# Graph network on one core: the first layer's sender rows gathered unscaled during the degree histogram, into a ring in SBUF

## What is computed

```python
h = relu(layernorm(x))
out_deg = clip(zeros(n).at[src].add(1), 1);  in_deg = clip(zeros(n).at[dst].add(1), 1)
agg = zeros_like(h).at[dst].add((h * out_deg ** -0.5)[src])
x = x + agg * in_deg ** -0.5

h = relu(layernorm(x))
n = ln(mlp(h));  e = ln(mlp(edge_attr_8))
for s in range(2):
    e = e + ln(mlp(concat([e, n[src], n[dst]])))
    agg = segment_sum(e, dst)
    n = n + ln(mlp(concat([n, agg])))
out = x + mlp(n)
```

## Time and profile before

| | |
|---|---|
| Median of 3 runs (lowest, highest) | 12392.23 us (12387.93, 12393.55) |
| Profiled execution: span | 12392.1 us |
| PE busy | 9269.5 us (75%) |
| PEld busy | 6879.9 us (56%) |
| DVE busy | 5309.1 us (43%) |
| ACT busy | 5441.9 us (44%) |
| POOL busy | 8911.3 us (72%) |
| Mean granted TensorE clock | 0.701 of full speed |
| HBM read, written | 616.95 MB, 249.33 MB |

### The profile page before, as it was taken

One profiled execution on the slowest core, in us unless ns is written; L12 is line 12 of the kernel. 1 busy time (PEld: TensorE's weight loads), 2 busy tenths in 40 slices (PEclk: granted clock), 3 DMA queues, 4 the chain that ended last, 5 costly groups with the idle time before them and its releaser, 6 DMA issues. The chain is left out here.

```text
span 12392.1 us, 209313 instructions
## 1 busy us (share of the span) xinstructions
PE 9269.5 (75%) x60787; PEld 6879.9 (56%) x60787; DVE 5309.1 (43%) x10581; ACT 5441.9 (44%) x8544; POOL 8911.3 (72%) x9488
## 2 busy tenths in 40 slices
PE   5687888788888867777777777776667677777776
PEld 4576666677777755555555555554444444444444
DVE  8844444444444434444444444443333333333333
ACT  1144444444444434444444444444444444444444
POOL 1277777777777767777777777776777777777776
PEclk8755555555555567777778788777777777777777
DMA  2122222222222223333334444442233333333332
GB/s 79 21 38 37 37 37 37 37 41 44 44 44 44 44 69 96 96 96 96 96 97 104 103 104 104 104 101 70 70 70 70 70 70 71 73 73 73 73 73 62
DMA packets 1513870, 857.80 MB, mean 69 GB/s; under 512 B 1044173, under 2 KB 1204574, under 8 KB 1512881
## 3 DMA queue, kind: packets, MB, share of 16 engines
q1 hardware_dynamic: 1115074, 571.64, 17.4%
q0 software_dynamic: 302816, 231.81, 11.7%
q10 hardware_dynamic: 95408, 47.86, 1.4%
HBM read 616.95 MB, written 249.33 MB: 70 GB/s over the span
## 5 line engine op out<-in xcount | busy, mean ns | idle before, releaser
L1803 POOL DMA_INDIRECT edge_blk_g<-sender_part,edge_blk_lst x6256 | 5909.6, 945 | 2000.4 <-issue 1904.5
L1403 POOL DMA_INDIRECT fl_gx<-sender_x,fl_lst x3128 | 2953.7, 944 | 1375.5 <-issue 951.9
L1859 PE MATMUL edge_blk_hps<-ident,edge_blk_g 128*128 128x128 f32 x6256 | 1244.4, 361 | 2066.6 <-DMA edge_blk_g<-sender_part,edge_blk_lst 2065.3
L1859 PEld LDWEIGHTS edge_blk_hps<-ident,edge_blk_g 128*128 128x128 f32 x6256 | 1058.8, 255 | 2818.4 <-DMA edge_blk_g<-sender_part,edge_blk_lst 2796.8
L1875 ACT ACT_TABLE_LOAD x1564 | 2006.6, 1283 | 60.2 <-ACTq L966 32.0
L1889 ACT ACTIVATE edge_blk_h<-edge_blk_hps,vecs 128x512 f32<-128x512 f32 x782 | 537.3, 687 | 2885.2 <-PE edge_blk_hps L1859 2875.2
L1948 DVE SCALAR_TENSOR_TENSOR agg<-edge_blk_aggps,vecs,agg 64x64 f32 x1564 | 442.3, 283 | 3102.6 <-PE edge_blk_aggps L1819 2641.8
L1854 PE MATMUL edge_blk_hps<-edge_blk_oha,edge_blk_win 128*128 128x512 f32 x1564 | 1137.9, 817 | 30.1 <-DMA edge_blk_win<-receiver_part 30.1
L1842 PEld LDWEIGHTS edge_blk_yps<-w_edge_blk,edge_blk_h 64*128 64x128 f32 x12512 | 1000.7, 239 | 244.2 <-issue 244.2
L1842 PE MATMUL edge_blk_yps<-w_edge_blk,edge_blk_h 64*128 64x64 f32 x12512 | 1122.7, 333 | 0.0
L1451 PE MATMUL fl_aggps<-fl_ohb,fl_gx 128*96 128x64 f32 x6256 | 1072.5, 365 | 13.8 <-DMA fl_gx<-sender_x,fl_lst 13.8
(11 more groups left out here) (279 smaller groups left out, 11497.4 us busy)
## 6 DMA issues: line engine op xcount, KB each, us to landing
edge_blk_e<-edge_state SPq DMA_DIRECT2D x782, 256.0 KB
edge_state<-fl_e SPq DMA_DIRECT2D x391, 256.0 KB
edge_blk_dlb<-local_dst SPq DMA_DIRECT2D x1564, 64.0 KB
edge_blk_g<-sender_part,edge_blk_lst POOLq DMA_INDIRECT x6256
edge_state<-edge_blk_new SPq DMA_DIRECT2D x391, 256.0 KB, 3.1
fl_gx<-sender_x,fl_lst POOLq DMA_INDIRECT x3128
edge_blk_win<-receiver_part SPq DMA_DIRECT2D x1564, 16.0 KB
fl_attr<-attr_slots SPq DMA_DIRECT2D x391, 32.0 KB
```

The source lines that it names most:

```text
L1403: pool.indirect_dma_start(out=gx[n.b][:, j % TILES, j // TILES, D:D + X_DIM], out_offset=None, in_=xg_d, in_offset=bass.IndirectOffsetOnAx ...
L1803: pool.indirect_dma_start(out=g[n.b][:, i, 64 * c:64 * c + 64], out_offset=None, in_=ps_d, in_offset=bass.IndirectOffsetOnAxis(ap=lst[n.b] ...
L1859: ins = nc.tensor.matmul(h_ps[n.half][:, P * i:P * i + P], g[n.b][:, i, :], ident[:, :], start=False, stop=i == TILES - 1)
```

## The change

**Order of the stages.** `load_weights` moves from GpSimd's part of `edge_lists` to its part of the set-up. The set-up writes `hx` to memory unscaled (`normed_x`), and the block ends only when that has landed. `scaled_senders` is gone; its arithmetic stands at the end of `edge_lists`.

**Lists.** The transposed source numbers and local destinations stay in SBUF for all rounds (`idx_all`, i32, and `loc_all`, bf16). `tile_lists` is gone with its stores and with all loads of lists, in layer one and in both edge steps.

**Ring.** `gr` holds 64 rounds of gathered rows. GpSimd fills it during `edge_lists`: rounds 0 to 47 out of the unscaled table, as soon as their block's lists exist, rounds 48 to 61 out of the scaled one, once that is in memory. In layer one it goes on from round 62, and from round 64 on it waits for the slot. A new step `take` on VectorE copies a round from the ring to `gx`. GpSimd's loops are unrolled over all rounds.

**Lookup.** The first 48 rounds have to be scaled in SBUF. Their digits are stored as bf16, and each round's are spread over the partitions by two DMAs. VectorE compares the high digits with the partition's number (`hot`), TensorE multiplies the result with the 98 x 128 table of factors, split into three bf16 parts (`look`, six matmuls of 512 columns), VectorE picks by the low digit (`pick`), TensorE sums over partitions with a column of ones (`total`, eight f32 matmuls), and every 16 rounds VectorE multiplies the ring's rows with the factors (`scale`).

```diff
+RING = 64
+LIST_BLOCKS = 3
+EARLY = LIST_BLOCKS * BLOCK_E // ROUND
+AHEAD = 62
+def every_round(pool, body, count_sb, first=0):
+    for n in range(first, FAST_ROUNDS):
+        body(n)
+    sort = pool.value_load(count_sb[0:1, 0:1], min_val=0, max_val=1)
+    with pool.If(sort > 0):
+        for n in range(FAST_ROUNDS, MAX_ROUNDS):
+            body(n)
+
+def gather_sender_x(pool, n, gr, idx_all, table, g_in):
+    if n >= QUAD:
+        pool.wait_ge(g_in[n % QUAD], n // QUAD * 128)
+    for j in range(8):
+        pool.indirect_dma_start(
+            out=gr[:, n % RING, j, :], out_offset=None, in_=table,
+            in_offset=bass.IndirectOffsetOnAxis(ap=idx_all[:, 8 * n + j:8 * n + j + 1].bitcast(U32), axis=0),
+        ).then_inc(g_in[n % QUAD], 16)
...
 # set-up
-                    sp.wait_ge(s_zeros, 64)
+                    sp.wait_ge(s_hx, 1)
+                    sp.dma_start(xh_d.rearrange("(p q) c -> p q c", q=P), hx[0:NHI, :, :]).then_inc(s_zeros, 16)
+                    sp.wait_ge(s_zeros, 80)
...
+                    pool.wait_ge(s_clear, len(zero_list))
+                    load_weights(pool)
...
 # edge_lists, GpSimd
-                load_weights(pool)
+                for n in range(AHEAD):
+                    if n < EARLY and n % per_block == 0:
+                        pool.wait_ge(lists_ok, n // per_block + 1)
+                    elif n == EARLY:
+                        pool.wait_ge(lists_ok, LIST_BLOCKS + 1)
+                        pool.wait_ge(rows_out, 32)
+                    gather_sender_x(pool, n, gr, idx_all, xh_d if n < EARLY else xg_d, g_in)
...
 # edge_lists, SP
+                def spread(r):
+                    if r >= 3:
+                        sp.wait_ge(picked_ok, r - 2)
+                    sp.dma_start(hi_bc[r % 3][0:NHI, :], digit_d[1, r:r + 1, :].broadcast_to([NHI, ROUND])).then_inc(bc_in[r % 3], 16)
+                    sp.dma_start(lo_bc[r % 3][:, :], digit_d[0, r:r + 1, :].broadcast_to([P, ROUND])).then_inc(bc_in[r % 3], 16)
...
 # edge_lists, VectorE, behind the histogram
+                def hot(r):
+                    dve.wait_ge(bc_in[r % 3], r // 3 * 32 + 32)
+                    if r >= 2:
+                        dve.wait_ge(z_ok, r - 1)
+                    v.tensor_scalar(hi_hot[r % 2][0:NHI, :], hi_bc[r % 3][0:NHI, :], part_f[0:NHI, 0:1], None,
+                                    ALU.is_equal).then_inc(hot_ok, 1)
+                def pick(r):
+                    dve.wait_ge(z_ok, r + 1)
+                    if r >= 2:
+                        dve.wait_ge(fac_ok, r - 1)
+                    v.scalar_tensor_tensor(picked[r % 2], lo_bc[r % 3][:, :], part_f[:, 0:1],
+                                           z_ps[r % 2][:, :, :].rearrange("p c e -> p (c e)"), ALU.is_equal, ALU.mult).then_inc(picked_ok, 1)
+                def scale(k):
+                    dve.wait_ge(fac_ok, per_block * k + per_block)
+                    for b in range(QUAD):
+                        dve.wait_ge(g_in[b], per_block // QUAD * (k + 1) * 128)
+                    rows = gr[:, per_block * k:per_block * k + per_block, :, :].rearrange("p r j c -> p (r j) c")
+                    v.tensor_tensor(rows, rows, fac_ps[k % 2][:, 0:P].rearrange("p (r j) -> p r j", j=1).broadcast_to([P, P, X_DIM]),
+                                    ALU.mult).then_inc(scaled, 1)
...
 # edge_lists, TensorE, behind the histogram
+                def look(r):
+                    pe.wait_ge(hot_ok, r + 1)
+                    if r >= 2:
+                        pe.wait_ge(picked_ok, r - 1)
+                    for c in range(2):
+                        for i in range(3):
+                            ins = nc.tensor.matmul(z_ps[r % 2][:, c, :], r_parts[0:NHI, i, :], hi_hot[r % 2][0:NHI, CHUNK * c:CHUNK * c + CHUNK],
+                                                   start=i == 0, stop=i == 2)
+                    ins.then_inc(z_ok, 1)
+                def total(r):
+                    pe.wait_ge(picked_ok, r + 1)
+                    k, at = r // per_block, 8 * (r % per_block)
+                    if k >= 2 and at == 0:
+                        pe.wait_ge(scaled, k - 1)
+                    for j in range(8):
+                        ins = nc.tensor.matmul(fac_ps[k % 2][:, at + j:at + j + 1], picked[r % 2][:, P * j:P * j + P], one_f[:, :],
+                                               start=True, stop=True)
+                    ins.then_inc(fac_ok, 1)
...
 # first_layer
-                    landed(sp, g_in, n.back(4), 128)
-                    held(sp, passed)
-                    wait(sp, oh_ok, n.back(4))
-                    sp.dma_start(lst[n.b][:, :], lists_d[bass.ds(n.n, 1)].rearrange("a p c -> (a p) c")).then_inc(list_in[n.b], 16)
...
+                def body(n):
+                    if n >= RING:
+                        pool.wait_ge(take_ok, n - RING + 1)
+                    gather_sender_x(pool, n, gr, idx_all, xg_d, g_in)
+
+                every_round(pool, body, count_sb, AHEAD)
...
+                def take(n):
+                    landed(dve, g_in, n, 128)
+                    held(dve, passed)
+                    v.tensor_copy(gx[n.b][:, :, :, D:D + X_DIM].rearrange("p i c d -> p c i d"),
+                                  gr[:, bass.ds((n.m & (RING // QUAD - 1)) * QUAD + n.b, 1), :, :].rearrange(
+                                      "p a (c i) d -> p (a c) i d", i=TILES)).then_inc(take_ok, 1)
...
                     finish(n.back(4))
+                    take(n.back(3))
...
 # edge_step
-                    indices(n)
                     operands(n.back(2))
                     store(n.back(6))
```

More of the change, by code:

```diff
@@ L121, in held @@
     eng.sem_inc(passed, 1)
-def rounds(eng, body, count_sb, first=1):
-    quads = load_count(eng, count_sb, "quads")
-    for m in range(first):
-        for b in range(QUAD):
-            body(Slot(m, b))
-    with eng.Fori(first, quads) as m:
-        for b in range(QUAD):
-            body(Slot(m, b))
-    return Slot(quads, 0)
+def every_round(pool, body, count_sb, first=0):
[13 more added lines that the diff above has]
+        ).then_inc(g_in[n % QUAD], 16)
 def rounds_and_nodes(eng, body, count_sb, first=1):
@@ L698, in edge_lists @@
         GT = 16
-        NHI = -(-(N_NODES + 1) // P)
         G = P // GT
@@ L755, in _ @@
                 store(blocks - 1)
-                sp.wait_ge(lists_out, blocks * 32)
+                sp.wait_ge(digits_out, LIST_BLOCKS * 32)
+                for r in range(3):
+                    spread(r)
+                for k, q in enumerate(half_cols):
+                    sp.wait_ge(rows_ok, k + 1)
+                    sp.dma_start(xg_d.rearrange("(p q) c -> p q c", q=P)[:, q, :], hx[0:NHI, q, :]).then_inc(rows_out, 16)
+                for r in range(3, EARLY):
+                    spread(r)
+                sp.wait_ge(lists_out, blocks * 16)
                 held(sp, passed)
+                sp.wait_ge(rows_out, 32)
             @block.scalar
@@ L832, in _ @@
                 blocks = load_count(dve, count_sb, "blocks")
-                body(0)
-                with dve.Fori(1, blocks) as k:
+                for k in range(LIST_BLOCKS):
+                    body(k)
+                with dve.Fori(LIST_BLOCKS, blocks) as k:
                     body(k)
@@ L840, in _ @@
+                hot(0)
+                for r in range(EARLY):
+                    if r + 1 < EARLY:
+                        hot(r + 1)
+                    pick(r)
+                    if r % per_block == 2 and r > per_block:
+                        scale(r // per_block - 1)
+                scale(LIST_BLOCKS - 1)
+                dve.wait_ge(scaled, LIST_BLOCKS)
             @block.tensor
@@ L1697, in _ @@
                     normed(last.back(k))
+                    take(last.back(k + 1))
                     add_sums(last.back(k + 2))
                     finish(last.back(k + 2))
+                take(last.back(1))
                 for k in (2, 1):
@@ L1796, in _, with body @@
             def _(pool):
[L1797 to L1800 removed]
+                def body(n):
+                    if n >= QUAD:
+                        pool.wait_ge(pre, n - QUAD + 1)
                     for j in range(8):
```

290 lines of the change are left out of this document (143 added, 147 removed).

## The result

| | before | after |
|---|---|---|
| Median (lowest, highest), 4 runs each | 12391.86 us (12387.93, 12393.55) | 12214.11 us (12201.35, 12236.74) |
| Profiled execution: span | 12392.1 us | 12207.6 us |
| Round 0, round 390 of layer one | 534.5, 4402.0 | 890.6, 4242.1 |
| First gather of the first edge step | 4483.7 | 4308.7 |

The ratio is 0.9859, 95% interval 0.9847 to 0.9871: 178 us less where 72 were forecast. The direction was right and the time lies in the range, at its lower end; the gain is two and a half times the forecast one. The profiled execution has 2.1 us outside its span.

What follows compares the result with a forecast made beforehand. GpSimd's gathers were taken to bind all three layers at 9.99 us a round. Gains of 418 and 8 us less 354 for the later round 0 gave 72 us less, 12,320 us from 12,392; range 12,190 to 12,450.

Steps and rivals of the forecast that it cites:

- Round 0: Start of layer one: at 888, 354 us later than before, as GpSimd must first issue 62 rounds of gathers.
- one gather a pair: Histogram: one gather passes with each pair of one-hots, plus one a block, 225 in all; chance 0.45.
- a cover of 7.0: Lookup of 48 rounds, 5 us each, hides under GpSimd's remaining gathers, which leave 7.0 us a round.
- Rivals 1 to 3: Histogram gathers: 1, starved, 12,539 us, chance 0.12; 2, no bf16 conflict, 12,213, 0.10; 3, in between, 12,256, 0.13.
- Part 1: Layer one: engines run at their own pace, 8.70 then 8.97 us a round, 3449 us against 3867.5; gain 418 us.
- rival 4: Layer one: TensorE gets 2.4 GHz and GpSimd's 3287 us bind; 162 us less, 12,158; chance 0.07.
- rival 5: Layer one: 192 late rounds stay at up to 9.99 us; up to 196 us back, 12,516, middle 12,418; chance 0.11.
- The new copy out of the ring: Layer one, VectorE: put at 0; 0.3 us a round, 117 us, if it came onto the chain.
- Part 3: Edge steps: still GpSimd's at 9.99 us a round; only the list load goes, 4 us a step, 8 in all.

Runs made afterwards that it cites:

- keys_psum: Changed kernel with the histogram one-hots' keys read as f32 from PSUM instead of bf16 from SBUF; one execution, 16207.83 us beside 15,669 for the kernel before.
- slots12: Changed kernel with the histogram's one-hots cut into 7 low and 5 high a block instead of 8 and 8; 1.0122 and 1.0127 of the kernel before.
- warm3: Changed kernel plus three bf16 matmuls an iteration of layer one into unread PSUM; 12155.11 us, 0.9796 of the kernel before; 0.9982 on another chip.
- after_again: The changed kernel once more, no edit, beside the kernel before on another chip; 12214.99 us, ratio 0.9855.
- ahead56: Changed kernel with 56 rounds gathered in the list block instead of 62; 12163.31 us, 0.981 of the kernel before; 0.9951 on another chip.
- no_early_again: Changed kernel without early gathers and lookup, all rounds gathered scaled in layer one; 12410.9 us, 1.0001 of the kernel before.
- best2_third: Changed kernel with slots12's cuts, warm3's matmuls, no empty 392nd round, and two bf16 table parts in the lookup instead of three; 1.0092 to 1.0098 of the kernel before.

## Why the prediction was right in its parts and wrong in its size

**Round 0.** Right, 890.6 for 888, and nearly in every part: one gather a pair, 225 of them in the histogram, 62 rounds done at 870 (forecast 874). Small terms were off and cancelled: the set-up cost 11 us and not 7, VectorE lost nothing to the gathers where I had put 10, and from GpSimd's last gather to round 0 it took 20 us and not 14. In the lookup 5.79 us stood for 5, under a cover of 7.0. By the Trainium skill (SBUF — State Buffer, Who interferes with whom) a VectorE instruction with two SBUF inputs contends with a GpSimd instruction that reads SBUF; the rule names no type. The traces agree for bf16: 1.72 us in the kernel after, 0.94 in keys_psum with one such input. Rivals 1 to 3 are out: gathers neither starved nor ran freely, and with both inputs in SBUF they went faster than one a pair only when slots12 made the one-hots longer.

**The engines' own pace, Part 1: this step failed.** It took 8.70 and 8.97 us, "both at 1.2 GHz", for all 390 rounds: 3449 us. They took 3351.5. The early rounds at 1.2 GHz are as forecast (8.75), and so are the late ones by their median (8.76), though not by their mean (9.26 for 8.97), which the rounds with node work raise. But 112 rounds had 2.4 GHz for a part. I had read in the windows of before that the clock stood at 0.51 to 0.55, and not asked what its few stretches at 2.4 GHz would be worth once GpSimd no longer hid them. That such stretches can come more often, and that this shortens the rounds, warm3 shows: three short matmuls take rounds 26 to 180 from 8.34 to 7.61 us. It is rival 4, with a chance of 0.07, in part: the clock rose in a tenth of the time, so that GpSimd's line, which rival 4 had as the bound, was nearly reached (last gather at 4197) and bound only in warm3. Its 12,155 us lie so near the 12,158 of the rival by some luck: 390 rounds took 3264.5 us for 3287, and what follows took 19 us more than the rival's sum has. The Trainium skill (TensorE: Matmul & The Clock Gate, Part 1) says that activity releases the throttle. The prediction said that the trace disagrees for this mix; the runs correct that: at 0.92 busy the share stays at 0.04 to 0.16, and with the three matmuls it is 0.48 in rounds 26 to 180.

**Late rounds (rival 5).** They sped up as the early ones did: 8.65 us a round over 192 rounds (1660.5 us, forecast 1722). The new copy out of the ring lay off the chain.

**Part 3, mis-sized.** 24.6 us and not 8. The list load gave 3.3. In and between the two steps and at the end another 9.5 were saved: with 392 rounds for 391 the gathers of a step take 6 and 9 us longer, but from the last of them to what follows, the next step or the end, 12 us less pass each time, as the last round is empty. The other 11.8 lie between round 390 and the first edge step, which are 66.6 us apart after and 81.7 before, with the list load. Where GpSimd binds, the last rounds' gathers are still to come when TensorE turns round 390; where the engines bind they are in the ring. The experiments show both: 65.7 us in after_again and 66.3 in ahead56_again, 84.4 in warm3_again and 83.5 in no_early_again, where GpSimd binds.

**The sum.** 516 - 356 + 25 = 184 for 418 - 354 + 8 = 72: a small difference of two large terms, of which one was off by a quarter of itself.

## What to carry to other kernels

When a change frees the engines of the one that binds, their own pace is not what the few free rounds of before show at the clock of before: ask what the stretches at 2.4 GHz were worth, and give that a term of its own. Short extra matmuls in a wait of TensorE can pay (60 us of 12,215 here), but only until the next line binds, so trim that line too. VectorE's two-input instructions let more gathers through when they are just longer than the period of what GpSimd issues beside them (1.27 against 1.25 us) and not just shorter; but no run here gained time by it, and on the chips where it was tried the kernel became slower. A change that makes GpSimd's stream denser has to be timed on both kinds of chip.

## What the runs showed of the hardware

- A gather (descriptor work of 0.94 us on GpSimd) that wants to start inside a VectorE instruction with both inputs in SBUF, bf16 too, starts when that ends: 1.72 us in the histogram. With one input in PSUM it isn't held (944 ns under instructions of 2.29 us). VectorE loses nothing (430.66 us of one-hots with 223 gathers beside them, 430.71 without).
- Reading the keys as f32 from PSUM instead of bf16 from SBUF makes a one-hot of 2048 elements 2.29 us instead of 1.22.
- More work can make TensorE faster: three bf16 matmuls of 256 columns a round, and rounds 26 to 180 take 7.61 instead of 8.34 us each, at a clock of 0.74 instead of 0.54. A round takes 8.73 us wholly at 1.2 GHz and 6.65 wholly at 2.4 GHz.
- On five of the six chips of the experiments the other engines stood still, VectorE for up to 75 us at a time (best2_third), while gathers were issued each 1.25 us, and not while they were issued each 2.02 us (ahead56); the kernel before takes 26 to 28% longer there. The cause is open.
